# A decoder layer with routed experts on one core: every piece at a new place in the engines' orders, other counts of filler matmuls, and TensorE instead of VectorE turning the rows of expert tiles 5 to 7

## The reference

```python
x = x + self_attention(layernorm(x))        # 16 heads of 16, 2-d rope on q and k, biases
x = x + cross_attention(ctx, ctx, layernorm(x), mask)   # keys = values = ctx, no q/k/v projections
y = layernorm(x)
p = softmax(y @ router_w.T + router_b + 0.1 * lang_weights)   # 8 experts
top_p, top_i = top_k(p, 2); top_p /= top_p.sum()
h = gelu(y @ w1[e] + b1[e])                 # 256 -> 1024
x = x + sum over the two chosen e of top_p * (h @ w2[e] + b2[e])  # 1024 -> 256
```

## Time and profile before

| | before |
|---|---|
| median of 3 runs | 722.53 us (719.61 to 723.65) |
| the profiled execution | 723.94 us, of which the span of its instructions 721.6 us |
| PE busy | 660.9 us (92% of the span) |
| DVE busy | 492.3 us (68%) |
| ACT busy | 431.6 us (60%) |
| POOL busy | 291.9 us (40%) |
| mean granted clock of TensorE | 0.976 of full speed |
| moved by DMA | 78.26 MB, mean 108 GB/s |

### The profile page before, as it was taken

The page is one execution under the profiler, slowest core; times in us unless marked ns, Lnnn a source line. Parts: engine busy times, 40 slices in busy tenths (PEclk is TensorE's granted clock), DMA queues, the critical chain, the costliest instruction groups (busy, mean ns, idle before and its releaser), DMA issues.

```text
span 721.6 us, 16087 instructions
## 1 busy us (share of the span) xinstructions
PE 660.9 (92%) x5012; PEld 521.1 (72%) x5012; DVE 492.3 (68%) x1355; ACT 431.6 (60%) x846; POOL 291.9 (40%) x547
## 2 busy tenths in 40 slices
PE   8678899999999999979968989899999999999996
PEld 4445576666767666646645677789999999999995
DVE  2396788686877777748853424677787878778781
ACT  3444657576676777757534765845665656565551
POOL 4233335254342464614173363544343333434322
PEclk9899999999999999989998999999999999999999
DMA  4546355455545555674796572133222212222221
GB/s 133 146 126 163 112 127 169 134 164 158 141 134 164 164 163 150 183 203 141 202 270 75 176 152 54 23 24 43 42 40 36 45 30 45 33 43 38 38 31 22
DMA packets 55843, 78.26 MB, mean 108 GB/s; under 512 B 15374, under 2 KB 45297, under 8 KB 54737
## 3 DMA queue, kind: packets, MB, share of 16 engines
q1 hardware_dynamic: 42441, 62.37, 31.4%
q0 software_dynamic: 8512, 10.26, 9.5%
q10 hardware_dynamic: 4808, 4.61, 2.7%
HBM read 54.52 MB, written 22.35 MB: 107 GB/s over the span
## 4 chain that ended last, share of the span: by engine, by line
PE 71%; DVE 8%; issue 6%; POOL 5%; ACT 4%; DMA 2%; another core or an unknown queue 1%; SPq 1%; ACTq 1%; DVEq 0%; POOLq 0%
PE attention_psum L753 18%; PE attention_psum L760 17%; PE attention_psum L745 8%; PE attention_psum L695 6%; PE attention_psum L714 5%; PE attention_psum L793 4%; PE attention_psum L650 3%; PE attention_psum L644 3%; PE attention_psum L639 3%; DVE neg_max L1236 2%; PE attention_psum L831 2%; POOL rstd L1414 1%; PE attention_psum L803 1%; POOL tmp L1414 1%
## 5 line engine op out<-in xcount | busy, mean ns | idle before, releaser
L1236 DVE TENSOR_REDUCE neg_max<-attention_psum 128x2 f32<-128x512 f32 x256 | 168.7, 683 | 61.7 <-PE attention_psum L695 54.1
L924 ACT ACTIVATE weights<-attention_psum 128x512 f32<-128x512 f32 x256 | 147.7, 596 | 90.9 <-PE attention_psum L714 63.7
L1020 ACT ACTIVATE weights<-attention_psum,b_sb 128x128 f32<-128x128 f32 x312 | 89.4, 370 | 105.1 <-PE attention_psum L753 102.5
L753 PEld LDWEIGHTS attention_psum<-over,v 128*128 128x128 f32 x1248 | 147.2, 194 | 6.5 <-DVE over L1288 3.5
L753 PE MATMUL attention_psum<-over,v 128*128 128x128 f32 x1248 | 148.1, 277 | 4.0 <-DVE over L1288 3.1
L760 PE MATMUL attention_psum<-weights 128*128 x624 | 143.2, 383 | 0.0
L1288 DVE STREAM_TRANSPOSE over<-over 32x64 f32<-32x64 f32 x544 | 128.2, 236 | 7.0
L1513 POOL DMA_INDIRECT out<-over x39 | 64.6, 1655 | 160.5 <-DVE over L1304 152.9
L760 PEld LDWEIGHTS attention_psum<-weights 128*128 128x128 f32 x624 | 116.8, 192 | 14.7
L695 PE MATMUL attention_psum<-weights 99*128 99x256 bf16 x512 | 100.2, 278 | 11.8 <-DVE neg_max L1236 11.0
L714 PE MATMUL attention_psum<-weights 102*128 102x256 bf16 (+1 forms) x512 | 103.1, 276 | 5.4 <-DMA weights<-maxT 4.6
(11 more groups left out here) (169 smaller groups left out, 743.0 us busy)
## 6 DMA issues: line engine op xcount, KB each, us to landing
parts<-weights SPq DMA_DIRECT2D x96, 128.0 KB
weights<-parts SPq DMA_DIRECT2D x64, 192.0 KB
weights<-parts SPq DMA_DIRECT2D x64, 128.0 KB
weights<-in_L_ffn_w SPq DMA_DIRECT2D x8, 1024.0 KB
weights<-parts SPq DMA_DIRECT2D x64, 64.0 KB
w_sb<-in_L_ffn_w SPq DMA_DIRECT2D x8, 512.0 KB
weights<-in_L_ffn_w SPq DMA_DIRECT2D x8, 512.0 KB
weights<-in_x SPq DMA_DIRECT2D x8, 256.0 KB, 3.1
```

Of the source, the lines that this page charges most:

```text
L753: last = pe.matmul(m.hT_bank[j % 2][:, c * P:(c + 1) * P], m.w1t[j % 2][:, k, c * P:(c + 1) * P], m.xT[j % 2][:, k, :], start=(k == 0), st ...
L924: act.activation(m.p[:, u % P_RING, :], m.b_bank[u % B_RING], ACT.Exp, scale=SCALE[ORDER[u // H][0]]).then_inc(m.b_free[u % B_RING], 1)
L1020: last = act.activation(m.hidT[n % HIDDEN][:, c, :], m.hT_bank[n % 2][:, c * P:(c + 1) * P], ACT.Gelu, bias=m.b1_sb[:, bass.ds(gelu_expert ...
L1236: v.tensor_reduce(m.neg_max[:, :, h:h + 1], m.a_bank[u % A_RING].rearrange("p (t k) -> p t k", t=T), AXX, ALU.max, negate=True).then_inc(m ...
```

## The change

No function is altered. What differs are the tables of places, the table of filler matmuls and one number:

```diff
-WARM = ((18, "turn", 0, 0), (4, "max", 0, 0, 0), (6, "stack", 0, 0, 0), (8, "max", 0, 0, 1), (14, "turn", 0, 1), (2,
...
+WARM = ((10, "top", 0, 0), (26, "turn", 0, 0), (2, "max", 0, 0, 0), (9, "stack", 0, 0, 0), (4, "max", 0, 0, 1), (30,
+        "turn", 0, 1), (2, "turn", 0, 2), (2, "qk", 0, 2, 1), (2, "max", 0, 3, 1), (8, "turn", 0, 4), (3, "max",
...
-W1_AT = (188, 194, 198, 235, 239, 241, 246, 252)
-W2_AT = (246, 246, 252, 253, 262, 269, 277, 275)
+W1_AT = (189, 186, 199, 235, 239, 241, 246, 257)
+W2_AT = (248, 240, 250, 258, 267, 270, 278, 278)
...
-        "w1t", 1), (278, "up_a", 0), (280, "up_b", 0), (281, "gather", 4), (281, "up_a", 1), (285, "gather", 5),
...
+        "up_a", 0), (277, "gather", 4), (278, "w1t", 1), (280, "up_b", 0), (282, "up_a", 1), (283, "w1t", 2),
...
-SQUARES = 5
+SQUARES = 8
```

More of the change, by code:

```diff
@@ L103 @@
         0), (-15, "v", 1))
-CROSS_AT = ((-38, "cx"), (-32, "ln_a", 1), (-29, "keys"), (-24, "ln_d", 1), (-18, "vcross"))
-BOTH_AT = ((-19, "stack", 0), (-19, "rest", 0), (-18, "mid", 0), (-17, "stack", 1), (-17, "rest", 1), (-17, "write", 0),
-        (-16, "mid", 1), (-13, "write", 1), (-12, "read", 0, 0), (-9, "read", 0, 1), (-7, "read", 1, 0), (-4,
-        "read", 1, 1), (8, "max_parts", 0), (11, "max", 0), (11, "max_rows", 0), (15, "max_parts", 1), (17,
+CROSS_AT = ((-38, "cx"), (-32, "ln_a", 1), (-26, "keys"), (-22, "ln_d", 1), (-16, "vcross"))
@@ L148 @@
-AFTER_SELF = ((18, "xbias"),)
-AFTER_CROSS = ((31, "ln_a", 2), (36, "ln_d", 2), (37, "rturn"), (38, "logits"))
-W1_AT = (188, 194, 198, 235, 239, 241, 246, 252)
-W2_AT = (246, 246, 252, 253, 262, 269, 277, 275)
-AFTER_BATCH = (((39, "softmax"), (39, "soft_exp"), (40, "choose"), (41, "count"), (41, "gate_exp"), (42, "gates"), (42,
+FIRST_AT = ((-31, "ln_a", 0), (-30, "ln_d", 0), (-29, "turn"), (-28, "qk_a", 0), (-27, "qk", 0), (-25, "qk_a", 1), (-24,
+        "qk", 1), (-23, "rope", 1), (-22, "v", 0), (-20, "rope", 0), (-19, "roped", 0), (-19, "roped", 1), (-18,
+        "v", 1), (-18, "stack", 0), (-17, "rest", 0), (-16, "stack", 1), (-15, "mid", 0), (-15, "rest", 1),
+        (-15, "write", 0), (-15, "mid", 1), (-15, "write", 1), (-12, "read", 0, 0), (-12, "read", 1, 0), (-4,
+        "read", 1, 1), (-3, "read", 0, 1))
@@ L154 @@
+AFTER_SELF = ((19, "xbias"),)
+AFTER_CROSS = ((31, "ln_a", 2), (36, "ln_d", 2), (37, "rturn"), (39, "logits"))
+W1_AT = (189, 186, 199, 235, 239, 241, 246, 257)
+W2_AT = (248, 240, 250, 258, 267, 270, 278, 278)
+AFTER_BATCH = (((39, "softmax"), (39, "soft_exp"), (40, "choose"), (41, "count"), (39, "gate_exp"), (42, "gates"), (42,
         "places"), (43, "counted"), (45, "table")), ((38, "softmax"), (39, "soft_exp"), (39, "choose"), (42,
-        "count"), (42, "gate_exp"), (43, "gates"), (43, "places")), ((40, "softmax"), (38, "soft_exp"), (40,
+        "count"), (40, "gate_exp"), (43, "gates"), (44, "places")), ((38, "softmax"), (37, "soft_exp"), (40,
```

84 lines of the change are left out of this document (42 added, 42 removed).

## The result

| | before | changed |
|---|---|---|
| median of 10 runs | 722.76 us (719.61 to 724.50) | 717.32 us (713.33 to 719.66) |
| ratio | | 0.9921, 95% interval 0.9899 to 0.9943 |
| profiled execution | 723.94, span 721.6 | 714.5, span 712.5 |

What follows compares the result with a forecast made beforehand. PE was taken as the bound, busy 660.9 of 721.6 us, with gains from idle time and half clock. Terms of -15.1 gave 708.8, 707.4 beside the median; 2 us for unseen waits made 709, range 701 to 718.

Steps and rivals of the forecast that it cites:

- The start: Up to 60 us: added fillers mostly hide in a 4.89 us wait, and regained full clock offsets their cost; -0.2 us.
- 60 to 303 us: Fillers removed where PE was busy, additions mostly hidden in waits, two waits ended by order alone; -3.2 us.
- The maxima: Near 305 to 312 us: moving a 512 KB load away makes u11's row-maxima DMAs land sooner, ending wait and half clock; -4.8 us.
- The start of the experts: 419 to 479 us: waits and half clocks go, partly because PE turns tiles 5 to 7 instead of DVE; -6.1 us.
- 366 to 399, and up to the turn of tile 0: Within the 303 to 419 us term of -0.8 us; the unnamed stall counted as unchanged, bounds of 4 either way.
- the 2 us kept for waits not foreseen: Added to the whole sum for new waits not seen, about a seventh of what is removed; 2 us.
- Rival 1: Row maxima still late or the experts' wait replaced, one term of 5 or 6 shrinking to 1 or 2; 713 to 715, chance 0.24.
- Rival 2: The unnamed stall of 376 to 387 us changes: gain to 700 to 703, chance 0.1; loss to 714 to 718, chance 0.08.
- Rival 3: Fillers are paid and waits return behind them: 724.1 us, no change, chance 0.06; up to 728.5, slower, chance 0.04.
- a long new wait: Sign of being wrong: behind ACT near 424 us, behind SP's other small DMAs, or a second unnamed one.
- the last term: The experts' start, 419 to 479 us; by the skill's transpose figures, a loss of about 1.7 us and no gain.

Runs made afterwards that it cites:

- a2: The changed kernel with the filler table of the kernel before (158 issued instead of 239), all else as changed; 716.60 us, ratio 0.9914.
- d4: The changed kernel with the fillers of the kernel before from slot 20 to 200 (27 fewer); 718.54 us, ratio 0.9899.
- b1: The kernel before with only the first three w1 loads moved, to slots 189, 186, 199; 721.61 us, ratio 0.9993.
- a3: The changed kernel with tiles 5 to 7 turned by DVE again; 718.55 us, ratio 0.9944.
- c1: The changed kernel with the w2 loads of experts 0 to 5 moved behind SP's loads of the lists; 718.95 us, ratio 0.9933.
- c2: The kernel before with w2 of experts 0 to 5 moved to slots 266 to 269, behind the lists; 731.18 us, ratio 1.0133.
- d1 to d4: Changed kernel, in turn: w2 of experts 2 to 5 behind lists; only expert 3's; first and last edits together; fewer fillers. 716.83, 716.03, 717.32, 718.54 us.
- e1: The changed kernel without the w2 loads of experts 0 to 5, all tiles using that of expert 7; 714.08 us, ratio 0.9875.
- e2: The kernel before without the w2 loads of experts 0 to 5, all tiles using that of expert 7; 723.44 us, ratio 1.0011.
- e4: The changed kernel unaltered, run again on another chip with a second profile; 716.74 us, ratio 0.9921.
- e3: The changed kernel with every w2 load cut into four (256 KB each, packets of 2 KB instead of 8); 716.46 us, ratio 0.9912.
- a1: The changed kernel with the last w1 load back at slot 252 and the first three w2 loads at 246, 246, 252; 716.49 us, ratio 0.9900.
- c3: The changed kernel with the scatters set two slots later, though they began no later (355.88 us against 355.95); 717.16 us, ratio 0.9906.
- c4: The changed kernel with w1t of tile 0 at slot 266 instead of 261; 719.09 us, ratio 0.9947.
- f1: The changed kernel with the two stores of cross unit 4 (output and rows) issued by SP instead of ACT; 715.15 us, ratio 0.9913.
- f2: The kernel before with the two stores of cross unit 4 (output and rows) issued by SP instead of ACT; 721.10 us, ratio 0.998.

## Why the prediction was wrong, point by point

**Two terms of the sum failed. The others were right in size; the two large ones were partly so by luck, since their reasons were wrong.**

*The start* (-0.2): the profiled pair shows -0.1, the means over the profiles -1.4. Full clock from 24 to 31 us, as forecast, and the wait of 4.89 fell to 1.44 with the turn at 28.07, for which 27.9 was said.

*60 to 303 us* (-3.2): measured +0.4, the first failed step. It was two sums. For order alone the forecast had -2.1 (the waits at 267 and 278), and a2 shows -0.6. For the fillers it had -1.1: 2.0 from the 18 taken away, and additions nearly free inside waits. a2 shows +1.1, 2.2 us from what was said. Two steps failed together: that fillers taken away where PE did not wait give 2.0, and that "the rest fits into waits of 0.8 to 1.7 us [...] and costs nothing". In the traces of a2 and of the changed kernel PE's idle time from u2 to u11 falls from 9.1 to 5.1 us with the fillers and its busy time rises from 209.1 to 214.2. How much one filler costs isn't settled: a2 has 57 there and takes 218.2, d4 has 53 and takes 218.9. The counts were short too: the trace has 39 added and 16 taken away up to 303 us where the forecast has 37 and 18, and from there to the turn of tile 0, beside the ten at the maxima, 13 more where it has 4.

*The maxima* (-4.8): u11 to u13 measured -4.7 and -3.9, half clock gone. The reason given was wrong. I said that the 512 KB load right ahead makes the landing slow. In the changed kernel no load stands there and the landing still took 4.75 us. The three DMAs were issued some 2 us sooner (303.84 in the chain, 305.84 before), where 1.04 was said, and so the last landed 2.0 sooner, at 310.42. With that alone, in a2, the row is 2.1 us shorter (52.3) and the wait 3.83; the other 2.6 come with the fillers: ten ahead of `cturn` keep PE busy until 309.94 (310.55 less its wait), and no half clock follows. So the size was met by luck: the landing didn't get faster, and the fillers, counted as a cost of 2.16, were what kept the clock. b1 fits the load as a cause in part (2.61 us without, and a new wait of 2.28 where the load went), so it may be one cause of several; which make the 4.75 stays open.

*The start of the experts* (-6.1): measured -7.3 and -5.2. The wait of 3.11 is gone with its half clock, and a new half clock near 424 did not come. But the reason was wrong: the forecast gave 3.1 + 1.7 us of it to the transposes that leave DVE, and a3, which keeps them on DVE, has 6.5 of the 7.3. `SQUARES` is worth 0 to 2 us, not told from noise; the places of the pieces, which bring DVE's routing and table sooner, did most. The 1.4 said for the wait at 445.25 didn't come, it is 1.11 and 1.42. The figure of 0.22 us of PE per tile holds: a tile turned by PE takes 7.24 us from `up_a` to `up_a`, and 7.03 without the 0.22 (the chain, tiles 5 and 6):

```profile
463.05 3.57 PE attention_psum L756 x32
466.62 3.46 PE attention_psum L763 x16
470.07 0.22 PE attention_psum L865 x2
470.29 3.57 PE attention_psum L756 x32
```

*366 to 399, and up to the turn of tile 0* (-0.8): measured +2.8 and +3.5, the second failed step, and the largest. "I count nothing for it, with bounds of 4 either way" took the stall of 8.3 us as a fixed cost that stays where it is. At the fourth head of u15 (389.24 us against 400.78) the changed kernel was 11.5 us ahead, in its second profile 7.2; at the turn of tile 0 1.6 and 2.0. What PE meets there is set by others: the last w1 load, the rows store, the list and rows of tile 0. In all twenty profiles the first lists are issued between 384 and 402 us and the turn of tile 0 starts between 401 and 412, whatever was won before. The changed kernel has 11 more fillers in this row, 2.4 us of work; whether they cost anything isn't shown, for a2 without them takes 63.1 us.

**What holds that stretch is not settled.** Shown: it appears in two forms. One is unnamed waits of ACT and DVE between 372 and 387 (before, c1, c2, d1 to d4, e1, e2, e4, and e3, where the issue of the rows store itself holds ACT for 5.5 us); the other a rows store that lands after 24 to 30 us, mostly with a w1 load that ACT waits for (after, a1 to a3, c3, c4, f1). Some executions have both (d4, e3, e4). b1 and f2 have neither in full; PE's turn of tile 0 comes 6 and 4 us sooner in them than in the kernel before, and their medians are 1.7 us lower, which is within the noise. Taking away one cause brought the other or a third. It is not the w1 load's place (a1), the place of `w1t` (c4), the packets' size (e3), or w2 alone (e1, e2), and ACT as the issuer isn't shown to be (f1, f2). The two forms part by the load on the DMA engines from 366 to 399 us: in the ten profiles with a late store their share is 0.79 to 0.99, while the unnamed waits come at any share, in e2 4.5 us of them at 0.19. So busy DMA engines may explain the first form and can't alone explain the second. What no run left out is the 16 scatters of 4-byte entries by GpSimd (L1441), since the tiles' lists come of them; whether they are the cause was not tried.

**The sum again.** 3.6 us too much from 60 to 303, 3.6 to 4.3 in the last stretch before the experts; the 2 us kept for waits not foreseen cover a quarter. The rest of the distance between the pair's 9.1 us and the medians' 5.4 is which executions were profiled. Rival 1 (713 to 715, chance 0.24) named the right kind, a wait in place of one removed, at the wrong places. Rival 2's loss, the stall of 376 to 387 changing (714 to 718, chance 0.08), is the one that came true by place and by time, though nothing had shown which way it would go. Rival 3 has a part in it: a2 shows that fillers counted as a gain from u2 to u11 cost. The text's test "a long new wait" was met, behind ACT, at 397 and not at 424.

No median is clearly below the changed kernel's; e1, which leaves work out, is lowest at 714.08.

## What to carry to other kernels

Before adding up gains along a kernel, find the points where it meets something that doesn't move with them, here a DMA-fed start of the next stage, and cap the sum there. Fillers and moved loads trade one wait for another. Don't book a filler as free: here 23 more, 5.0 us of work, put 1.1 us on one stretch, and ten ahead of a wait that a DMA ends won 2.6 in the next. And take two profiles of each kernel before pricing a stall that the trace cannot name: here it moved or vanished from one execution to the next.

## What the runs showed of the hardware that was not expected

A store of 256 KB landed 23.5 to 29.7 us after its issue in ten executions (24.96 in the changed kernel, with the DMA engines busy at a share of 0.91 and moving 156 GB/s from 366 to 399 us; 29.5 in c4, at 0.95); others have 10.8 to 13.3 for the same store (c1 at 0.49, b1 at 0.77, f2 at 0.74). The last of three DMAs of 4 KB around 306 us landed after 4.86 us before, 4.75 in the changed kernel, 3.52 in a2 and 2.61 in b1, the last three with no load right ahead.

The Trainium skill ("VectorE: DVE Perf Modes", The three transpose paths) gives 390 ns for TensorE and 311 for VectorE for a 128x128 bf16 transpose, from which the prediction worked out, beside its sum, an estimated loss of about 1.7 us for the last term. The rows decide otherwise for these float32 tiles: PE pays 0.22 per tile, and with the transposes back on DVE (a3) the kernel is no faster (718.55, 0.9944).
